# An attention period that was two score tiles, two products of maxima and one block of 64-column tiles is issued in two halves

## What is computed

```
x = x + 0.5 * ffn(layernorm(x))     # 8 experts, top 2 by a sigmoid gate, and a shared expert
x = x + attn(layernorm(x))          # 16 heads of 64; attn normalises again and adds its own residual
x = x + 0.5 * ffn(layernorm(x))
```

```
scores = einsum('bhqd,bhkd->bhqk', q, k) * scale
attn = softmax(scores)
out = einsum('bhqk,bhkd->bhqd', attn, v)        # then @ w_out.T + residual
```

## Time and profile before

| | us |
|---|---|
| median of three runs | 4295.57 |
| lowest, highest | 4295.1, 4296.23 |
| the profiled execution, its time | 4299.85 |
| the profiled execution, its span | 4298.1 |

### The profile page before, as it was taken

The page is one execution under the profiler, slowest core; times in us unless marked ns, Lnnn a source line. Parts: engine busy times, 40 slices in busy tenths (PEclk is TensorE's granted clock), DMA queues, the critical chain, the costliest instruction groups (busy, mean ns, idle before and its releaser), DMA issues. The chain is left out here.

```text
span 4298.1 us, 65988 instructions
## 1 busy us (share of the span) xinstructions
PE 3978.9 (93%) x24896; PEld 2241.8 (52%) x24896; DVE 2674.3 (62%) x3451; ACT 3004.5 (70%) x3792; POOL 3046.9 (71%) x1642
## 2 busy tenths in 40 slices
PE   7999969999999999999999999999999999879999
PEld 6888824444444444444444444444444444358888
DVE  5556547666666666766666666666766666345653
ACT  4444438877777787778777777878787778635444
POOL 3444438878788887888788788878887888724444
PEclk9999979999999999999999999999999999979999
DMA  3333121112211211121122112111211121123331
GB/s 106 105 119 109 60 94 58 50 51 65 65 59 57 70 57 53 54 82 50 50 65 65 53 63 70 50 53 58 85 50 50 55 75 54 42 92 119 119 106 63
DMA packets 194366, 301.13 MB, mean 70 GB/s; under 512 B 51486, under 2 KB 102400, under 8 KB 193408
## 3 DMA queue, kind: packets, MB, share of 16 engines
q1 hardware_dynamic: 194048, 296.92, 21.4%
HBM read 201.92 MB, written 26.74 MB: 53 GB/s over the span
## 5 line engine op out<-in xcount | busy, mean ns | idle before, releaser
L1001 DVE TENSOR_REDUCE atNM<-atPS 128x2 f32<-128x1024 f32 x1024 | 1208.5, 1220 | 798.2 <-PE atPS L817 794.5
L1084 POOL TENSOR_TENSOR atACC<-atACC,atPT 128x1024 f32<-128x1024 f32 x512 | 1291.2, 2522 | 65.0 <-ACT atPT L939 10.7
L939 ACT ACTIVATE atPT<-atPS 128x1024 f32<-128x1024 f32 x1024 | 993.1, 1022 | 197.1 <-PE atPS L838 191.1
L930 ACT ACTIVATE atPS<-atSH 128x1024 f32<-128x1024 f32 x1024 | 1008.6, 1021 | 32.3 <-DMA atSH<-atMD 24.8
L849 PE MATMUL atPO<-atPT,atV 128*64 128x512 f32 x4096 | 978.0, 598 | 0.0
L1084 POOL TENSOR_TENSOR atACC<-atPT 128x1024 f32<-128x1024 f32 x256 | 621.5, 2428 | 144.6 <-PE atOT L860 127.7
L817 PE MATMUL atPS<-atKH,atQH 64*128 64x512 f32 x2048 | 463.1, 450 | 163.0 <-ACT atPT L939 137.1
L1063 POOL TENSOR_TENSOR atVT<-atVT,atSIN 128x512 f32<-128x512 f32 x256 | 349.7, 1366 | 325.3 <-DMA atVT<-atR 325.3
L849 PEld LDWEIGHTS atPO<-atPT,atV 128*64 128x64 f32 x4096 | 282.9, 138 | 482.2 <-issue 476.1
L838 PE MATMUL atPS<-atQH,atKL 64*128 64x512 f32 x2048 | 469.1, 454 | 28.2 <-ACT atPS L930 28.1
L817 PEld LDWEIGHTS atPS<-atKH,atQH 64*128 64x128 f32 x2048 | 194.7, 185 | 412.6 <-ACT atPT L939 348.7
(11 more groups left out here) (246 smaller groups left out, 6549.4 us busy)
## 6 DMA issues: line engine op xcount, KB each, us to landing
atVT<-atR SPq DMA_DIRECT2D x512, 128.0 KB, 2.0
atSH<-atMD SPq DMA_DIRECT2D x128, 512.0 KB, 4.5
f1GB<-f1GD SPq DMA_DIRECT2D x128, 256.0 KB, 6.8
atRSUM<-atRD SPq DMA_DIRECT2D x128, 256.0 KB, 4.1
f2GB<-f2GD SPq DMA_DIRECT2D x128, 256.0 KB, 7.0
f1XB<-in_x SPq DMA_DIRECT2D x5, 1024.0 KB, 5.5
x<-f1XB SPq DMA_DIRECT2D x5, 1024.0 KB, 8.2
f2XB<-x SPq DMA_DIRECT2D x5, 1024.0 KB, 5.4
```

The source lines that it names most:

```text
L930: act.eng.activation(PS[ring.of[("score", n, t, j)]][:, :, :], SH[t][:, :, :], ACT.Copy).then_inc(filled[j % 2].sem)
L939: act.eng.activation(PT[k % NPT][:, :, :], PS[ring.of[step]][:, :, :], ACT.Exp, scale=SCALE).then_inc(grown.sem)
L1001: dve.eng.tensor_reduce(NM[:, q // 4, :, q % 4, t], PS[ring.of[step]][:, :, :], AX.X, ALU.max, negate=True).then_inc(most_out.sem)
L1084: pool.eng.tensor_tensor(total[:, :, :], begun[:, :, :], PT[k % NPT][:, :, :], ALU.add).then_inc(gathered.sem)
```

## The change

Before, a period read: both scores, both products, the early steps, both fills, both attends, the gathers, the late steps. Now it reads: one score, one product, the early steps, one fill, one attend; then the other score, product, fill and attend; then gathers and the late steps. Nothing is added or removed. Since the banks go round in the order of the steps, the two uses in the middle exchange their banks' predecessors.

```diff
@@ -682,8 +682,9 @@
                 mosts = [("most", m + 1, q, i) for i in range(2)] if 0 <= m + 1 < NN else []
                 n2, r2 = divmod(g + 1, PER)
                 fills = [("fill", n2, r2 // 4, 2 * (r2 % 4) + i) for i in range(2)] if 0 <= n2 < NN else []
-                order += begin.get(g, []) + scores + mosts + early.get(g, []) + fills + attends
-                order += [("gather",) + s[1:] for s in attends if s[3] % 4] + late.get(g, []) + end.get(g, [])
+                gathers = [("gather",) + s[1:] for s in attends if s[3] % 4]
+                order += begin.get(g, []) + scores[:1] + mosts[:1] + early.get(g, []) + fills[:1] + attends[:1]
+                order += scores[1:] + mosts[1:] + fills[1:] + attends[1:] + gathers + late.get(g, []) + end.get(g, [])
 
             def events(*names):
                 return [step[1:] for step in order if step[0] in names]
```

## The result

The changed kernel takes 4370.89 us (median of 4 runs, 4369.32 to 4375.05) against 4295.9 us for the kernel before, measured beside it: a ratio of 1.0177, 95% interval 1.0164 to 1.0189. It is slower, as forecast, and inside the range; the sum behind the forecast was +36 us, and the change cost twice that, 75 us.

What follows compares the result with a forecast made beforehand. TensorE was taken as the bound, busy 93% of the span, with ScalarE and GpSimd at 80% and more. Terms -113 + 60 + 53 + 37 + 24 - 25 = +36 us gave about 4332, stated as 4335 us; range 4225 to 4430.

Steps and rivals of the forecast that it cites:

- TensorE's own time: Every period: the second product's wait goes, one more turn is added; 4.38 to 4.16 us, -113 us over 512 periods.
- The row of maxima: After r = 1 and r = 5: ScalarE's row copy stands behind the second fill, delaying the next early step; +60 us.
- The copy of Q and the clock: Head boundaries: the next head's first product waits for ScalarE's copy of Q, +53 us; halved clock after such waits, +24.
- VectorE against GpSimd: Rotations on VectorE held up by GpSimd's sums now delay reductions and fills: +37 us, half of 74.
- The full price of 74 us: Port rule taken at every rotation: each collision of VectorE with GpSimd's sums counted, +74 in place of +37.
- Given back elsewhere: Where ScalarE normalises the next batch, 7 batches of 3 periods: the second product's wait for an exponential shrinks, -25 us.
- TensorE's gain stays: Rival, chance 0.24: waits on ScalarE are absorbed, under 1.7 us per head together; faster, 4190 to 4287 us.

Runs made afterwards that it cites:

- small sums: GpSimd's sums over the exponentials cut to 16 of 512 columns, in the changed kernel (4322.11 us) and in the kernel before (4275.78 us).

## Why the prediction was right, and where it was off

The direction and the mechanism were right: TensorE's own time fell and the queue of ScalarE took back more than that. Term by term:

- *TensorE's own time*, forecast -113 us. The wait went and the turn to fp32 work costs 0.32 to 0.33 us, as read from the earlier trace rows. The step that failed is the price of one more run of fp32 steps in each period, in the sum 2 x (0.80 + 0.32 + 0.86 + 0.10) = 4.16 us. The turn back does cost 0.10, but the attend before it is 0.91 and not 0.43 x 2 = 0.86 when it opens such a run: 0.15 us per run beyond its steps, and it comes twice. The rows of the kernel before had it (0.91 from raise to attends in the earlier trace rows; 1.77 us for four steps in the earlier trace rows, not 1.72); in the 1.86 us of the old period I had taken it for "slack for the fill". The period without single steps takes 4.27 to 4.29 us, not 4.16, so the term is 0.11 x 512 = -56 us. The run with the attend between the products, which has the same turns, is 71 us faster with all that follows from it; it includes what the waits at the normalisation gave back.
- *The row of maxima*, forecast +60 us. 0.30 us in the traces for my 0.47, thus 38 us of waiting. But removing it gained 4 us alone, within the noise, and next to nothing that shows beside the copy of Q. As a term of a sum it was over-sized in any case; the two runs with the row moved do not give its price, since the move brought a wait of its own, that of the transpose for VectorE.
- *The copy of Q and the clock*, forecast +53 and +24. The product's start was off by 0.15 us in 7.82, and the clock did fall behind such waits. Moving the copy gave 97 us, of which 5 are to be had in the old order too: some 91 us for 77 forecast. How much of this is clock was not separated by a run of its own. The mean granted clocks bound it: 0.978 before and 0.973 in the changed kernel make up to (1 - 0.973) x 4367.6 - (1 - 0.978) x 4298.1 = 23 us for the change as a whole, near the 24 forecast. That 13 of 24 waits would be followed by half clock (I had said 6 of 10) was a guess that held, as nothing in the rows gave this share.
- *VectorE against GpSimd*, forecast +37. 75 - 46 = 29 us, with some 10 us of uncertainty from the intervals: right in size. Half of 74 was no more than a middle between two bounds, so the closeness is in part luck, and as said, some 7 of the 29 can be GpSimd's own lateness. The full price of 74 us was too much, but not because collisions are rare. The mean rotation takes 1.41 us in the changed kernel and 0.76 with the small sums. Most of what they delay was not waited for; how much each costs was not separated. In the changed kernel with small sums period 1 even grew by 16 us, so part of the gain went into a longer wait for Q.
- *Given back elsewhere*, forecast -25, was not tested by a run of its own. In the traces, the first four periods of the heads where ScalarE normalises are shorter by 0.6 to 5.7 us in each of 7 batches, 25 us in all. Some 3 of these are TensorE's own 0.11 us a period, which leaves 22.

With what the runs and traces show, -56 + 38 + 91 + 29 - 22 = +80 us, against 75 measured. That fits closer than its terms are known: they overlap, and with 4 us for the row, as its removal gave, the sum would be +46. What the forecast had wrong in the main is one number, 0.05 us per run of fp32 steps, twice in each of 512 periods, which is 51 us; that the other errors nearly balanced is luck.

Of the rivals, the one that ended on the other side (TensorE's gain stays) had the right kind of condition, that the waits on ScalarE stay under TensorE's gain, though with 56 us of gain the bound is 0.9 us per head and not 1.7. One move on ScalarE's queue brought it about.

## What to carry to other kernels

When a step is cut in halves to remove a wait on the busiest engine, follow the other engines' queues: here each half's fill came to depend on a reduction of the same half, and one copy, last in ScalarE's queue, was waited for with half a period's work standing behind the waiting matmul. Split only what waited (here one attend between the two products, 1.6% faster) and leave the order of the engine that is 80% busy alone. When an operation comes a thousand times, read its whole cost, from entry to return, from the same kind of place in the same trace; 0.05 us is then 50 us.

## What the runs showed that I had not expected

A wait on TensorE can cost more than its length. Behind a wait of 2.44 us the granted clock was 0.51 for 3.40 us in the changed kernel, and 0.50 for 6.80 us behind one of 2.45 us in the kernel with the row moved; behind a wait of 1.01 us it stayed at 1. A change that gained 0.3 us in 128 periods was worth 4 us in all, in part for this, and in part because the step that it moved then waited for another engine's queue. And one instruction of 1.06 us, moved past two others in 1 of 8 periods, was worth 2.3% in one order of the same work and 0.16% in the other.
